# Two gated attention blocks on one core: queues reordered ahead of both attentions, and part of layer 1's queries moved into the feed-forward

## The reference

```python
x = x + tanh(g_xattn[0]) * L0_xattn(layernorm(x), ctx, ctx, ...)   # softmax attention, bias -0.1*|t - t'|
x = x + tanh(g_ffn[0])   * L0_ffn(layernorm(x), ...)               # relu(x W1 + b1) W2 + b2, ternary W1 and W2
x = x + tanh(g_xattn[1]) * L1_xattn(layernorm(x), ctx, ctx, ...)   # relu on q, k and v, softmax attention
x = x + tanh(g_ffn[1])   * L1_ffn(layernorm(x), ...)               # top-1 of 4 experts, gelu, layer norm
```

## Time and profile before

| | |
|---|---|
| median of three runs | 805.82 us (805.3, 805.82, 812.23) |
| the profiled execution | 808.54 us |
| its span, first to last instruction | 806.7 us |
| mean PEclk | 0.936 |
| busy: PE, DVE, ACT, POOL | 722.7, 582.0, 451.1, 296.5 us |
| stretches of the span | projections to 85.0, layer 0's attention to 269, feed-forward 323 to 402, its end and layer 1's queries to 439, layer 1's attention to 637, experts to the end |

### The profile page before, as it was taken

The page is one execution under the profiler, slowest core; times in us unless marked ns, Lnnn a source line. Parts: engine busy times, 40 slices in busy tenths (PEclk is TensorE's granted clock), DMA queues, the critical chain, the costliest instruction groups (busy, mean ns, idle before and its releaser), DMA issues.

```text
span 806.7 us, 12425 instructions
## 1 busy us (share of the span) xinstructions
PE 722.7 (90%) x4224; PEld 443.1 (55%) x4224; DVE 582.0 (72%) x1126; ACT 451.1 (56%) x968; POOL 296.5 (37%) x348
## 2 busy tenths in 40 slices
PE   5897599999999898899966999989999899999992
PEld 3443244444443466697733444444436489899991
DVE  5473689999992369454775899979993647877775
ACT  2322378888888453765312788868884433333330
POOL 2131155555555233765300000256442344343313
PEclk9898699999999999999976899989996899999997
DMA  8399435555545423001352145432201222111100
GB/s 301 113 188 220 126 125 175 183 175 181 186 147 214 151 59 105 1 1 53 94 165 58 42 132 181 150 112 80 80 3 55 80 93 87 48 49 46 43 16 22
DMA packets 51358, 87.54 MB, mean 109 GB/s; under 512 B 8597, under 2 KB 16791, under 8 KB 51296
## 3 DMA queue, kind: packets, MB, share of 16 engines
q1 hardware_dynamic: 44320, 72.06, 28.8%
q0 software_dynamic: 4576, 11.54, 5.5%
q10 hardware_dynamic: 2400, 3.15, 1.1%
HBM read 45.29 MB, written 41.63 MB: 108 GB/s over the span
## 4 chain that ended last, share of the span: by engine, by line
PE 69%; DVE 14%; SPq 4%; DMA 3%; POOL 3%; ACT 3%; issue 2%; POOLq 0%; DVEq 0%; ACTq 0%
PE ps_out L719 14%; PE ps_wide L598 8%; PE ps_a L705 8%; PE ps_wide L904 6%; PE ps_out L927 6%; DVE row_max L1403 5%; PE ps_a L527 5%; PE ps_misc L705 3%; PE ps_a L840 3%; SPq L443 2%; PE ps_a L916 2%; PE ps_wide L693 2%; PE ps_out L854 2%; PE ps_misc L854 2%; POOL hid_lo L1263 1%
## 5 line engine op out<-in xcount | busy, mean ns | idle before, releaser
L1403 DVE TENSOR_REDUCE row_max<-ps_wide 128x2 f32<-128x1024 f32 x256 | 301.5, 1220 | 31.4 <-PE ps_wide L598 25.1
L1029 ACT ACTIVATE probs<-ps_a 128x512 f32<-128x512 f32 (+1 forms) x418 | 199.8, 521 | 44.1 <-PE ps_a L705 36.2
L598 PE MATMUL ps_wide<-stack_k,stack_q 48*128 48x512 f32 x512 | 189.8, 468 | 19.2 <-DVE row_max L1403 14.1
L705 PE MATMUL ps_a<-stack_q,stack_k 62*128 62x512 f32 (+3 forms) x418 | 149.9, 422 | 12.2 <-ACT probs L1029 8.8
L719 PE MATMUL ps_out<-probs,vals 128*17 128x512 f32 x1024 | 139.3, 619 | 0.5 <-POOL probs L1222 0.5
L598 PEld LDWEIGHTS ps_wide<-stack_k,stack_q 48*128 48x128 f32 x512 | 89.5, 194 | 65.3 <-DVE row_max L1403 37.4
L1029 ACT ACTIVATE probs<-ps_misc 128x512 f32<-128x512 f32 (+1 forms) x222 | 114.2, 514 | 19.3 <-PE ps_misc L705 18.7
L1222 POOL TENSOR_TENSOR probs<-probs,fixes_sb 128x512 f32<-128x512 f32 x64 | 82.1, 1282 | 80.8 <-ACT probs L1029 80.8
L705 PEld LDWEIGHTS ps_a<-stack_q,stack_k 62*128 62x128 f32 (+1 forms) x418 | 65.8, 194 | 75.4 <-ACT probs L1029 40.8
L705 PE MATMUL ps_misc<-stack_q,stack_k 62*128 62x512 f32 (+3 forms) x222 | 96.9, 437 | 1.5 <-ACT probs L1029 1.5
L1207 POOL TENSOR_SCALAR max_neg<-row_max 128x16 f32<-128x16 f32 x32 | 9.3, 290 | 157.3 <-DVE row_max L1403 136.6
(11 more groups left out here) (211 smaller groups left out, 1309.4 us busy)
## 6 DMA issues: line engine op xcount, KB each, us to landing
rows_sorted<-blank SPq DMA_DIRECT2D x17, 1040.0 KB, 5.0
planes_k<-planes SPq DMA_DIRECT2D x32, 256.0 KB, 4.1
planes_q<-planes SPq DMA_DIRECT2D x32, 256.0 KB, 3.6
stack_q<-planes_q SPq DMA_DIRECT2D x64, 128.0 KB, 2.8
stack_k<-planes_k SPq DMA_DIRECT2D x64, 128.0 KB, 2.8
w_raw<-in_L_W SPq DMA_DIRECT2D x6, 1024.0 KB, 6.2
stack_q<-planes_q SPq DMA_DIRECT2D x64, 64.0 KB, 2.7
stack_k<-planes_k SPq DMA_DIRECT2D x64, 64.0 KB, 2.6
```

The costliest lines, as they stand in the source:

```text
L598: mm(raw_slot(l, ("pair", g, p))[:, i * S:(i + 1) * S], stack_q[at, slot(g, c) + q * P:slot(g, c) + (q + 1) * P], stack_k[at, slot(g, c):s ...
L705: mm(score_slot(("tile", n))[:, start:end], stack_k[at, slot(g, c) + k * P:slot(g, c) + (k + 1) * P], stack_q[at, slot(g, c) + start:slot( ...
L1029: do(probs[n % PROBS[l]][:, j, start:end], score_slot(("tile", n * TILES + t))[:, start:end], ACT.Exp, scale=0.25).then_inc(exp_done, 1)
L1403: v.tensor_reduce(row_max[:, g % 2, :, p], raw_slot(l, ("pair", g, p))[:].rearrange("p (i k) -> p i k", i=2), AX, ALU.max).then_inc(sem(f" ...
```

## The change

It reorders the queues and moves memory; the arithmetic stays.

- **Raws 14 pairs ahead** (AHEAD) in both layers: 14 pairs stand before attention, pairs 14 + 8g to 21 + 8g beside group g. So the last two pairs of group g + 1 lie in k = 0 of group g, and its `split_maximum` comes on POOL behind the first `fix` of group g.
- **Prologue row by row.** SP loads key stacks 0 and 1 behind the store of the first keys, query stacks behind their own store, stores a row's planes ahead of further loads, and loads stack 3 last. ACT's queue issues `load_inputs` one row at a time and `load_rest` in row 2, between its key copies and `turned_out`. POOL clears one stack slot, reads the constant rows once at the start, and copies them seven times within SBUF in row 1.
- **Layer 1's queries.** The first half of `hid0` of even rows gets memory of its own (`hid_low`), as does the queries' source (`turned_x`). `turn_n2(0)` and `queries1(0)` run amid the third row (f = 3 and 4) through the wide bank `pw[0]`; stacks 0 and 1 are loaded before the last row's third step, with five pairs in that row, one behind the turn of row 1's queries, one behind each `down0(3, q)`, and four among the last queries.
- **Spread loads.** `load_last` is one DMA a group from group 5 on; b1 is cleared, loaded and split in groups 0, 1 and 2; expert weights go two pieces a group from group 5 on, their loads from group 1 on.
- In the end stretch, pairs 126 and 127 fall in group 14's k = 0, so DVE does two reductions ahead of `normal(3, 0)`.

```diff
+AHEAD = 2 * PAIRS - 2
+FIRST_MAX = 12
-WEIGHTS_FROM = 6
+WEIGHTS_FROM = 5
+PIECES = 2
+        def hidden0(b, part_, f):
+            if b % 2 == 0 and f < FC // 2:
+                return hid_low[part_][:, f, :]
+            return hid0[b % 2, part_][:, f, :]
...
@@ SP, layer 0 @@
                     store_planes("k", 0)
+                    planes_left(sp, 0, C)
+                    for g in range(RING - 2):
+                        load_stacks(g, "k")
                     store_planes("q", 0)
                     planes_left(sp, 0, 2 * C)
-                    for g in range(RING - 2):
-                        load_stacks(g)
-                    for b in range(1, B):
+                    load_stacks(0, "q")
+                    store_planes("k", 1)
+                    load_stacks(1, "q")
+                    store_planes("q", 1)
+                    for b in range(2, B):
                         store_planes("k", b)
                         if b == B - 1:
                             send_maximum(0)
+                        else:
+                            load_stacks(RING - 2, "k")
                         store_planes("q", b)
                         if b < B - 1:
-                            load_stacks(RING - 3 + b)
-                    load_rest()
+                            load_stacks(RING - 2, "q")
+                    load_stacks(RING - 1)
@@ SP, layer 1 @@
+                    planes_left(sp, 1, B * C)
+                    for g in range(RING - 2):
+                        load_stacks(g, "k")
                     store_planes("q", 0)
-                    sp.wait_ge(sem("down0_done"), (B - 1) * QT)
                     planes_left(sp, 1, (B + 1) * C)
                     for g in range(RING - 2):
+                        load_stacks(g, "q")
+                    sp.wait_ge(sem("down0_done"), (B - 1) * QT)
+                    for g in range(RING - 2, RING):
                         load_stacks(g)
                     store_planes("q", 1)
-                    for g in range(RING - 2, RING):
-                        load_stacks(g)
@@ PE @@
-                    ahead = g + BEHIND
...
+                            ahead, p = divmod(AHEAD + g * PAIRS + 2 * k + c, PAIRS)
...
-                if b >= 2:
-                    queries1(b - 2)
+                    if b == 2 and f == 3:
+                        turn_n2(0)
+                    if b == 2 and f == 4:
+                        queries1(0)
+                    if b == B - 1 and f >= 3:
+                        first_raws(1, f - 3, 1)
+            turn_n2(1)
+            first_raws(1, 5, 1)
+            queries1(1)
             for q in range(QT):
                 down0(B - 1, q)
-                if q > 0:
-                    first_raws(1, q * (q - 1) // 2, q)
-            queries1(2, (6, 8, 12))
+                first_raws(1, 6 + q, 1)
+            turn_n2(2)
+            queries1(2, (10, 11, 12))
             first_maximum(1)
-            queries1(3, (12, 13, 16))
+            turn_n2(3)
+            queries1(3, (12, 13, 14))
@@ ACT, layer 0's projections @@
+                if b == 2:
+                    load_rest()
...
                 turned_out("n0", b)
+                if b < 2:
+                    load_inputs(b + 2)
@@ POOL, attention @@
                     if l == 0:
-                        for k in range(QT):
+                        fix(g * QT)
+                    if g + 1 < G:
+                        split_maximum(l, g + 1)
+                    if l == 0:
+                        for k in range(1, QT):
                             fix(g * QT + k)
...
+                    if l == 1 and g == 0:
+                        clear_bias()
+                    if l == 1 and g == BEHIND:
+                        split_bias()
+                    if l == 1 and 0 <= g - WEIGHTS_FROM < E * QT // PIECES:
+                        for n in range(PIECES * (g - WEIGHTS_FROM), PIECES * (g - WEIGHTS_FROM + 1)):
                             expert_weights(*divmod(n, QT))
...
@@ POOL, layer 0's projections @@
+                if b == 1:
+                    pool.wait_ge(sem("rows_in0"), 16 * N_ATT)
                     for i in range(2):
+                        for rows, n in zip(constant_rows(i), (NB, MP + NB)):
+                            pool.dma_start(rows[:, S:].rearrange("r (n t) -> r n t", t=S),
+                                           rows[:, 0:S].unsqueeze(1).broadcast_to([n, RING * 2 - 1, S])).then_inc(sem("rows_in0"), 16)
@@ DVE, last feed-forward rows @@
+                    if b == B - 2 and q > 0:
+                        first_maxima(1, 2 * q - 2, 2 if q < QT - 1 else 1)
+                    if b == B - 1:
+                        dve.wait_ge(sem("down0_added"), b * QT + q + 1)
+                        v.bn_stats(stats[:, b * QT + q, :], x[:, b * QT + q, :]).then_inc(sem("stats"), 1)
+                        first_maxima(1, 6 + q, 1)
+                    if q == 0 and b > 0:
+                        normal2(b - 1)
...
+            aggregate(2, B - 1, 1e-5)
+            normal2(B - 1)
             query_low(1, 2, 0)
-            first_maxima(1, 6, 2)
+            first_maxima(1, 10, 1)
             query_low(1, 2, 1)
-            first_maxima(1, 8, 4)
-            normal2(B - 1)
+            first_maxima(1, 11, 1)
             query_low(1, 3, 0)
             first_maxima(1, 12, 1)
             query_low(1, 3, 1)
-            first_maxima(1, 13, 3)
+            first_maxima(1, 13, 1)
```

More of the change, by code:

```diff
@@ L322, in raw_items @@
         def raw_items(l):
-            for g in range(G + BEHIND + 2):
-                if l == 1 and g == G + 1:
+            for m in range(AHEAD):
+                if m == FIRST_MAX:
+                    yield ("maximum", 0)
+                yield ("pair", *divmod(m, PAIRS))
+            for g in range(G):
+                if l == 1 and g == G - 1:
                     for what, b in (("n3", 0), ("n3", 1), ("logits", 0), ("count", 0), ("logits", 1), ("count", 1)):
@@ L328, in raw_items @@
                 for p in range(PAIRS):
[L329 to L334, removed]
+                    if p == PAIRS // 2 and g >= BEHIND:
+                        yield ("out", g - BEHIND)
+                    if AHEAD + g * PAIRS + p < G * PAIRS:
+                        yield ("pair", *divmod(AHEAD + g * PAIRS + p, PAIRS))
+            for g in range(G - BEHIND, G):
+                yield ("out", g)
         def score_items():
@@ L398, in _, with load_last, load_bias @@
                     sp.dma_start(dst, src).then_inc(signal, 16)
[L399 to L414, removed]
+            def load_last(n):
+                moves = ((w_mo_raw[:], part(a["L1_Wo"])), (w_router[:], part(a["L1_Wr"])),
+                         (bias_mo[:], a["L1_bo"].partition_broadcast(P)),
+                         (gamma[:], a["gamma"].partition_broadcast(P)), (beta[:], a["beta"].partition_broadcast(P)),
+                         (table[:], a["table"]), (sums[:], a["sums"]))
+                sp.dma_start(*moves[n]).then_inc(sem("w_last"), 16)
+            def load_bias():
                 sp.wait_ge(sem("b1_cleared"), 1)
@@ L1047, in _, with load_inputs, load_rest @@
             act.wait_ge(loaded_keys, 16 * N_KEYS)
-            for b in range(1, B):
+            def load_inputs(b):
                 for dst, src in (context_in(b), rows_in(b)):
                     nc.scalar.dma_start(dst, src).then_inc(sem(f"loaded_in{b}"), 16)
+            load_inputs(1)
+            def load_rest():
+                for dst, src in (
+                    (w_o[:], part(a["L0_Wo"])), (gates_raw[:], a["gates"].partition_broadcast(P)),
+                    (bias_o[:], a["L0_bo"].partition_broadcast(P)), (bias_2[:], a["L0_b2"].partition_broadcast(P)),
+                    (b1_cols[:], a["L0_b1"]), (fixes[:], a["fixes"]), (order[:], a["order"]),
+                ):
+                    nc.scalar.dma_start(dst, src).then_inc(loaded_rest, 16)
             for b in range(B):
```

183 lines of the change are left out of this document (104 added, 79 removed).

## The result

The changed kernel takes **797.75 us** (median of four, 792.33 to 803.2) where the kernel before takes 805.56 (four, 801.45 to 812.23): a ratio of 0.990, 95% interval 0.985 to 0.994. Forecast were 778 and the range 766 to 794, so the change is worth 8 us instead of 28. The profiled execution is the longest of the four (803.2, span 801.4), so its span is 5.3 us shorter than before's, not 8.

A forecast was written before the change was run, and what follows sets the result against it. Losses were placed in four stages of waits and low clock, not PE's busy share. Prologue -13.7, transition -13.6, spread loads -4.4 and end +2.5 summed to -29.2, 776.6 from the median; forecast 778, range 766 to 794.

The forecast's parts named there:

- Prologue (a) to (c), -13.7: Prologue: row 3 ends 5.1 us earlier after 2.6 for `load_rest` on ACT; the 8.6 us wait for late loads goes.
- if the broadcast, moved to row 1, holds up the loads of query stack 0 and the stores there as it does now in row 2, +5 on it: Prologue row 1: its gain falls to -8.7, time 783; one of the first two rivals 0.25, both 0.08.
- the second rival: Transition to layer 1: DVE and a cold clock leave -6 instead of -13.6, 786; one of first two rivals 0.25.
- Transition, -13.6: Feed-forward to layer 1's group 1: scores start 12.2 us earlier, group 0 gains 1.4; bounds -9.2 and -17.6.
- queries amid the third row: Feed-forward's third row: projections cost PE 3.7 us anywhere; a 0.69 us wait and the restart go, -1.2.
- four tiny ones, 0.7: DVE's four tiny operations in `normal(2, 2)`, before layer 1's scores, counted at 0.7 us together.
- Spread loads, -4.4: Layer 1's groups 7 and 8 fall from 26.6 us to 11.1 each: -4.4, between -3 and -5.
- layer 0's steady groups, 0: Layer 0: 14 pairs ahead instead of 16 costs nothing; at the upper end 14 groups lose 0.3 each, +4.
- the 0.3 us of cover for the split: Layer 0's groups: the split of the maxima behind the first `fix` ends 0.3 us before PE needs it.
- End, +2.5: Layer 1's group 14: two reductions ahead of `normal(3, 0)` delay DVE 2.4 us: +2.5, from +1 to +5.
- the better end of the prologue: Prologue: -17 if `load_rest` is hidden and row 1 also gains the 2 us PE waits for first stacks.
- that of the transition: Transition to layer 1: the more favourable bound of its -13.6 forecast, given as -17.6.

The follow-up runs named there:

- both_16: Changed kernel with constant rows broadcast from DRAM in row 2, POOL's roots at their old place, layer 1 at 16 pairs ahead: 777.92 us, ratio 0.960 to the kernel before.
- both: Changed kernel with constant rows broadcast from DRAM in row 2 and POOL's roots of the second norm at their old place: 782.87 us, ratio 0.968 to the kernel before.
- rows_late: Changed kernel with its SBUF to SBUF broadcast of the constant rows issued in row 2 instead of row 1: 791.73 us, ratio 0.983 to the kernel before.
- rows_before: Changed kernel with the constant rows as they were, broadcast from DRAM by POOL in row 2: 788.35 us, ratio 0.979 to the kernel before.
- rows_dram_1: Changed kernel with the constant rows broadcast from DRAM, but in row 1 of the prologue: 797.03 us, ratio 0.985 to the kernel before.

## Why the prediction was wrong

- **Prologue (a) to (c), -13.7: right, but for the broadcast.** With the rows back in row 2, the eight profiles put group 1 of layer 0 at 87.4 to 91.8 where before had 105.0: -13.2 to -17.6, around or beyond the term. `load_rest` on ACT, costed at 2.6 us, cost less: rows 2 and 3 of the changed kernel take 34.2 us together (53.3 to 87.5), where 37.5 were forecast.
- **The step that failed first** is the sentence "if the broadcast, moved to row 1, holds up the loads of query stack 0 and the stores there as it does now in row 2, +5 on it". The mechanism was seen, given a quarter of the chance together with the second rival, and underpriced: it costs 9.4 us of time (8.6 by the ratios), 9 to 13 in profiles. In the earlier trace rows it took 10.8 us of everything; the 5 is half of that, and the prediction gives no working for the half. In row 1 PE's next work was the very stack that SP was about to load, so the whole length came onto the path: a wait of 11.3 us. I also took a copy without DRAM for a cheaper one; in row 1 it is 3.4 us dearer in the first scores' start.
- **Transition, -13.6: the term "queries amid the third row" failed.** It has -1.2, "since `up0(2, 4)` covers it", and nothing for the normalising of rows 0 and 1 that these queries and the last row's pairs wait behind on DVE. The "four tiny ones, 0.7" stand in the sum for row 2, and there they hold, with 0.64. For rows 0 and 1 they take 4.9 each, beside POOL, and PE waits 2.7 and 2.2 us where the sum has no wait. The change moves the roots ahead of the next row's low halves; I looked at who waits for the roots, not at what then runs on POOL beside DVE. With the roots back the transition takes 182.6 to 184.0 against 196.3, -12.3 to -13.7. That this meets -13.6 is in part luck, since a wait of 2.1 us that the sum does not have is still in it. The Trainium skill (SBUF — State Buffer, "Who interferes with whom") has the rule that a VectorE instruction with two SBUF inputs contends with a GpSimd instruction that reads SBUF, and that the one that comes second is blocked for the whole length of the first. The trace agrees, by 1.24 and 1.21 beside POOL against 0.17 and 0.16 a microsecond later; the rule was there to be weighed against this change. The second rival (786) had the sign, by a backlog of DVE's own work, which is not what happened.
- **Spread loads, -4.4, and layer 0's steady groups, 0: right** (-4.3 and +0.2), with the 0.3 us of cover for the split: `max_cols` does not make PE wait in layer 0's steady groups.
- **End, +2.5: mis-sized.** Measured +4.3 in group 14 and +9.4 to the end of the span; in time 5.0 (both_16 against both). The upper end given was +5, if the clock fell sooner. That its size fits the time is luck: the clock fell 12 us into the group, as before, and stayed at 1.2 GHz for 34 us instead of 20. The term has PE's work 2.4 us later and no longer slow stretch behind it.

The sum itself has slips that do not move the forecast: the better end of the prologue is -18.3 by its terms, not -17, that of the transition -17.8, not -17.6, layer 1's scores would start 26 us earlier, not 27, and nothing leads from 776.6 to 778.

The three together, 9.4, 3.2 and 5.0 us, make 17.6 of the 19.8 that separate 778 from 797.75 (16.8 with the first by the ratios). The version without them takes 0.960 to 0.967 of the kernel before (three measurements), which is 773 to 779 where before takes 805.6.

## What to carry to other kernels

Do not price a background transfer by what it cost where it stood: ask which load is issued behind it and who waits for that, and reckon with its whole length. When an instruction is moved on one engine, list what now runs at that moment on the other engines, not only who waits for it. Where the tail of a stage is already tight, giving back two units of lead can cost more than it saved earlier, here 5 us, with a longer stretch at the lower clock behind it.

## What the runs showed of the hardware

- POOL's copy of 0.75 MB of rows from SBUF to SBUF into 52 partitions, issued in row 1, goes with 6.8 to 9.3 us for SP's next four issues (four profiles), where such four take 2.5 us without it. With 0.85 MB from DRAM in the same place these four take 2.5 us and the four stores at 40 us take 10.8, where they take 3.1 to 3.7 or, with ACT's input loads early, 6.4 to 6.9.
- DVE's operations on 128x4 take 1.2 us beside POOL's subtractions of 128x512 and 0.16 without. The one-input `TENSOR_SCALAR` at 355.10 is held just as long as those with two, and the rule cited above speaks of two.
- PE waited 2.70 to 2.72 us ahead of the first queries' transposes in seven profiles. In six of them the clock then read 1.2 GHz for 3 to 7 us, from between 0.7 us before the wait's end and 1.3 us after it; in rows_late it stayed at 2.4 GHz. The transposes took 1.97 us where the drop came ahead of them (changed, rows_before, rows_dram_1) and 1.09 to 1.30 in the other four, and with 14 pairs ahead the first kind has transitions of 187.6 to 190.6 us, the second of 184.4 and 186.0.
